# Chosen experts: where the next expert's turns and first products stand

## The reference

```python
xg = flat_x[topk_idx]
g = jnp.einsum('ecd,eid->eci', xg, Wg)
u = jnp.einsum('ecd,eid->eci', xg, Wu)
h = jax.nn.gelu(g, approximate=False) * u
eo = jnp.einsum('eci,edi->ecd', h, Wd)
eo = eo * topk_weight[..., None]
flat_out = jnp.zeros_like(flat_x).at[topk_idx.reshape(-1)].add(eo.reshape(-1, d))
```

## Time and profile before

| | |
|---|---|
| median of 3 executions | 4346.72 us (4342.63 to 4351.96) |
| the profiled execution: its own time | 4346.94 us |
| its span in the trace | 4345.3 us |
| TensorE matmuls busy | 3717.2 us, 86% of the span |
| VectorE busy | 2360.1 us, 54% |
| ScalarE busy | 1462.4 us, 34% |
| GpSimd busy | 1491.4 us, 34% |
| mean granted clock of TensorE | 0.915 of full speed |
| first turn of the chosen experts | 3586.20 us after the span's start |
| last down products of them begin | 4271.84 us |

### The profile page before, as it was taken

How to read it: one execution, slowest core, us unless ns; L and a number is a source line. 1 busy time by engine, 2 the same in 40 slices (tenths; PEclk the granted TensorE clock), 3 DMA queues, 4 the chain that set the end, 5 groups by cost and what they waited for, 6 DMA issues and landing times. The chain is left out here.

```text
span 4345.3 us, 55566 instructions
## 1 busy us (share of the span) xinstructions
PE 3717.2 (86%) x18610; PEld 1746.6 (40%) x18699; DVE 2360.1 (54%) x3948; ACT 1462.4 (34%) x2133; POOL 1491.4 (34%) x1279
## 2 busy tenths in 40 slices
PE   8989999998999689997699266476997989999994
PEld 3412222222333333333455255233555465555552
DVE  5579999964554135554722549655893661111113
ACT  2237777772333223333123124111452311111111
POOL 0042222234666216665156013133551322222221
PEclk9979999999999899999799576788997989999997
DMA  4543232311110431102422712233452113333323
GB/s 167 195 75 73 60 76 59 77 22 63 39 42 10 155 136 39 39 25 89 145 80 84 246 40 88 100 91 104 132 159 94 41 57 112 99 93 100 94 80 87
DMA packets 321435, 387.39 MB, mean 89 GB/s; under 512 B 56208, under 2 KB 248993, under 8 KB 319713
## 3 DMA queue, kind: packets, MB, share of 16 engines
q1 hardware_dynamic: 269376, 305.23, 22.5%
q0 software_dynamic: 31776, 57.19, 5.6%
q10 hardware_dynamic: 20096, 22.55, 1.5%
HBM read 240.68 MB, written 135.76 MB: 87 GB/s over the span
## 5 line engine op out<-in xcount | busy, mean ns | idle before, releaser
L590 DVE TENSOR_REDUCE modulated_mx<-modulated_ring 128x1 f32<-128x512 f32 x1024 | 651.4, 683 | 51.8 <-PE modulated_ring L497 45.9
L574 ACT ACTIVATE modulated_probs<-modulated_scores 128x1024 f32<-128x1024 f32 x512 | 496.1, 1021 | 181.5 <-PE modulated_scores L518 181.4
L2995 DVE TENSOR_TENSOR expert_h<-expert_gelu,expert_bank 128x512 f32<-128x512 f32 x128 | 88.1, 688 | 390.3 <-PE expert_bank L2963 387.5
L527 PE MATMUL modulated_acc<-modulated_probs,modulated_v 128*32 128x512 f32 x2048 | 273.6, 606 | 0.6 <-ACT modulated_probs L574 0.6
L497 PE MATMUL modulated_ring<-modulated_k,modulated_q 64*128 64x512 bf16 x1024 | 239.4, 399 | 34.1 <-DMA modulated_v<-scratch_v 23.0
L2923 POOL DMA_INDIRECT scratch_acc<-expert_y,expert_idx x64 | 101.1, 1580 | 482.2 <-DVE expert_y L3000 440.1
L518 PE MATMUL modulated_scores<-modulated_q,modulated_k 128*128 128x512 bf16 x945 | 255.6, 383 | 10.3 <-issue 5.4
L929 POOL TENSOR_TENSOR causal_total<-causal_total,causal_probs 128x1024 f32<-128x1024 f32 x96 | 225.7, 2351 | 86.9 <-ACT causal_probs L850 85.9
L929 POOL TENSOR_TENSOR meta_total<-meta_total,meta_probs 128x1024 f32<-128x1024 f32 x96 | 225.6, 2350 | 86.9 <-ACT meta_probs L850 85.9
L2963 PE MATMUL expert_bank<-expert_xT,expert_wg 128*128 128x512 f32 x512 | 243.2, 597 | 7.8 <-ACT expert_xT L2975 7.8
L872 DVE TENSOR_REDUCE meta_mx<-meta_maxima 128x2 f32<-128x1024 f32 x120 | 146.0, 1217 | 183.7 <-PE meta_maxima L756 183.7
(11 more groups left out here) (465 smaller groups left out, 6754.0 us busy)
## 6 DMA issues: line engine op xcount, KB each, us to landing
expert_wg<-x_WgT SPq DMA_DIRECT2D x16, 1024.0 KB, 4.9
expert_wu<-x_WuT SPq DMA_DIRECT2D x16, 1024.0 KB, 7.0
expert_wd<-x_WdT SPq DMA_DIRECT2D x16, 1024.0 KB, 5.2
modulated_k<-scratch_k_part SPq DMA_DIRECT2D x192, 64.0 KB, 2.9
modulated_q<-scratch_q_part SPq DMA_DIRECT2D x192, 64.0 KB, 3.0
scratch_v<-proj_v SPq DMA_DIRECT2D x8, 1024.0 KB, 6.5
modulated_v<-scratch_v SPq DMA_DIRECT2D x16, 512.0 KB, 4.5
scratch_M<-steps_snap SPq DMA_DIRECT2D x16, 512.0 KB, 3.2
```

The source lines that it names most:

```text
L527: last = nc.tensor.matmul(acc[32 * j:32 * j + 32, :], vs[g % SLOTS][:, t, j, :], probs[u % NPROBS][j // 2][:, j % 2, :], start=(t == 0), s ...
L574: nc.scalar.activation(probs[u % NPROBS][i][:], sc[i][:], ACT.Exp, scale=SCALE).then_inc(s_exp, 1)
L590: V.tensor_reduce(mx[h % 2][:, x // 2, 1 - j % 2, j // 2, x % 2:x % 2 + 1], ring[bank_of["max", 4 * m + j]][:], AX.X, ALU.max).then_inc(s_ ...
```

## The change

The jobs stand in another order. For each expert: g and u of f = 1 to 6; the other expert's turns; g and u of f = 7; the other expert's g 0 and u 0; the down products. For j = 1 "the other" is expert 0 of the next pair. What has no predecessor, the turns, g 0 and u 0 of expert 0, stands ahead of the loop; the last pair, which has no successor, is written out behind a loop of 7, with `tell` in the place of the missing jobs. `begin` gives the semaphores their credit up to the place in the list where that work starts.

```diff
         bank_of = lambda job: BANK[job[1]](job[2])
+        turns = lambda j: [(j, "turn", m) for m in range(KD)]
+        start_of = lambda j: [(j, "g", 0), (j, "u", 0)]
+        FIRST = turns(0) + start_of(0)
         jobs = []
         for j in range(2):
-            jobs += [(0, "turn", m) for m in range(KD)] if j == 0 else []
-            jobs += [(j, k, f) for f in range(FT) for k in ("g", "u")]
-
-            jobs += [(1, "turn", m) for m in range(KD)] if j == 0 else []
+            jobs += [(j, k, f) for f in range(1, FT - 1) for k in ("g", "u")]
+            jobs += turns(1 - j) + [(j, "g", FT - 1), (j, "u", FT - 1)] + start_of(1 - j)
             jobs += [(j, "d", a) for a in range(CT)]
+        LAST_D = [x for x in jobs if x[0] == 1 and x[1] == "d"]
+        lag = lambda x: int(x in FIRST)
+        spot = lambda steps: steps.names.index(next(x for x in FIRST if x in steps.names))
...
+        def begin(eng, steps):
+            eng.sem_inc(steps.sem, spot(steps))
+            steps.at = spot(steps)
...
-            def gather(i, j):
-
-                mm.wait(pool, i, (j, "turn", KD - 1), back=1)
+            def gather(i, j, first=False):
+                if not first:
+                    mm.wait(pool, i, (j, "turn", KD - 1), back=1 + int(j == 0))
...
+            begin(pe, mm)
+            for job in turns(0):
+                work(-1, job, 0, True)
+            act_s.wait(pe, -1, (0, "turn", KD - 1))
+            for kind in ("g", "u"):
+                mm.tell(pe, (1, kind, FT - 1))
+            for job in start_of(0):
+                work(-1, job, 0, True)
+            dve_s.wait(pe, -1, (0, "u", 0))
+            for job in LAST_D:
+                mm.tell(pe, job)
+            with pe.Fori(0, I_ - 1) as i:
+                for job in jobs:
+                    work(i, job, i + lag(job), False)
+            for job in jobs:
+                if job in FIRST:
+                    if job == (0, "turn", 0):
+                        dve_s.wait(pe, I_ - 1, (1, "u", FT - 2))
+                    if job == (0, "g", 0):
+                        dve_s.wait(pe, I_ - 1, (1, "u", FT - 1))
+                    mm.tell(pe, job)
+                else:
+                    work(I_ - 1, job, I_ - 1, False)
```

More of the change, by code:

```diff
@@ L2926, in scatter @@
                 freed[j].tell(pool, "y")
-            gather(0, 0)
+            gather(0, 0, first=True)
             with pool.Fori(0, I_ - 1) as i:
@@ L2940, in _ @@
             pe.wait_ge(s_made, 2)
[L2941 to L2953, removed]
-                    taken(before).wait(pe, i, before, back)
[L2955 to L2965, removed]
@@ new lines, in work @@
+            def work(i, job, e, ahead):
+                j, kind, m = job
+                out = bank[bank_of(job)]
+                if (kind, m) == ("turn", 0):
+                    gathered[j].wait(pe, e)
+                if (kind, m) == ("g", 0):
+                    act_s.wait(pe, i, (j, "turn", KD - 1))
+                    loaded[j].wait(pe, e)
+                if (kind, m) == ("d", 0):
+                    dve_s.wait(pe, i, (j, "u", FT - 1))
+                if not ahead:
+                    before, back = user_before(jobs, bank_of, jobs.index(job))
+                    taken(before).wait(pe, i, before, back)
+                if kind == "turn":
+                    for a in range(CT):
+                        last = nc.tensor.transpose(out[:, a * P:(a + 1) * P], xg[j][:, a, m * P:(m + 1) * P], ident[:])
+                elif kind == "d":
+                    for f in range(FT):
+                        last = nc.tensor.matmul(out[:, 0:D], h[j][:, f, m * P:(m + 1) * P], wd[j][:, f, :], start=(f == 0), stop=(f == FT - 1))
+                else:
+                    for kd in range(KD):
+                        last = nc.tensor.matmul(out[:], (wg if kind == "g" else wu)[j][:, kd, m * P:(m + 1) * P], xT[j][:, kd, :],
+                                                start=(kd == 0), stop=(kd == KD - 1))
+                mm.done(last, job)
@@ new lines, in work @@
+            def work(i, job, ahead):
+                j, kind, m = job
+                if kind == "turn":
+                    mm.wait(act, i, job)
+                    if not ahead:
+                        mm.wait(act, i, (j, "u", FT - 1), back=j)
+                    act_s.done(nc.scalar.activation(xT[j][:, m, :], bank[6 + m][:], ACT.Copy), job)
+                if kind == "g":
+                    mm.wait(act, i, job)
+                    if not ahead:
+                        before = (j, "u", m - 2) if m >= 2 else (1 - j, "u", FT - 2 + m)
+                        dve_s.wait(act, i, before, back=int((m >= 2 and j == 0 and m - 2 == 0) or (m == 1 and j == 0)))
+                    act_s.done(nc.scalar.activation(gel[m % 2][:], bank[m % 2][:], ACT.Gelu), job)
@@ new lines, in _ @@
+            begin(act, act_s)
+            for job in turns(0):
+                work(-1, job, True)
+            act_s.wait(act, -1, (0, "turn", KD - 1))
+            act_s.tell(act, (1, "g", FT - 1))
+            work(-1, (0, "g", 0), True)
+            with act.Fori(0, I_ - 1) as i:
+                for job in jobs:
+                    work(i, job, False)
+            for job in jobs:
+                if job in turns(0):
+                    if job == (0, "turn", 0):
+                        act_s.wait(act, I_ - 1, (1, "g", FT - 2))
+                    act_s.tell(act, job)
+                elif job != (0, "g", 0):
+                    work(I_ - 1, job, False)
```

41 lines of the change are left out of this document (27 added, 14 removed).

## The result

| | before | changed |
|---|---|---|
| median of 5 runs each, us | 4342.63 (4339.7 to 4351.96) | 4326.35 (4322.84 to 4330.98) |
| ratio, 95% interval | | 0.9959 (0.9945 to 0.9974) |
| profiled execution, span | 4345.3 | 4329.3 |
| first load of the stage issued to its last down products | 698.67 (3573.17 to 4271.84) | 682.71 (3574.19 to 4256.90) |
| granted clock, mean | 0.915 | 0.915 |

The stage is 15.96 us shorter in the trace, where 13.7 were predicted, and the span 16.0 us. The profiled execution of the changed kernel took 4330.98 us, the longest of its five.

The account below looks back on a forecast made before the run. TensorE was taken as the bound, with about 16 us idle. Gains of 16.4 less 2.6 at the edges and 0.1 for the gather made 13.7 us: 4346.94 - 13.7 - 0.2 = 4333.0, range 4328 to 4341.

Parts of the forecast that it names:

- Both stalls: TensorE's waits for xT copies ahead of gates (7.8 us gain) and expert_h ahead of down products (7.7 us) go.
- The pause ahead of the last pair's end: Last iteration: a wait for expert_h of f = 6 in the turns' place, 1.10 us plus 0.1 for increments.
- The gather's cover: Next gather ready 19.5 or 19.8 us after the down products' end, turns at 20.6; cover about 1 us.
- the one case at the edge: One gather ready 20.7 us after the down products' end, its turns due at 20.6; at most 0.1 us booked.
- The first loads' help: Prologue: asking for expert 1's weights after the first turns could gain 0 to 2.8 us; taken as 0.
- The clock: Rival: the prologue's new pause loses the risen clock again for 6 us, costing 3 us: 4336; chance 0.03.
- the rivals: Gather slightly late (0.07) or late enough to be slower (0.05), switches costing as much (0.09), clock falling in prologue (0.03).
- the switches: Rival: turns cost the full 1.11 us, up to down 0.2 per expert; net 9 us, 4338; chance 0.09.
- 4346.94 - 13.7 - 0.2 = 4333.0: Before's profiled time, less the net gain of 13.7 us, and 0.2 for lying above the median of 4346.72.
- A block of turns that nobody waits for: Eight turns on TensorE per expert, followed without a wait: between 0.88 and 1.11 us, taken as 1.00.
- The slow start behind a wait: Gate job behind the copies' wait takes 1.82 us in place of 1.72; 0.10 booked at seven boundaries.
- The prologue: Ahead of the loop TensorE waits for the first expert_h, 1.1 us, plus 0.3 for increments: 1.4 us.

Follow-up runs that it names:

- e1: Before with only the turns moved ahead of the last gate and up products; stage 696.54 us, median 4342.19 us, ratio to before 0.9999.
- e4: Changed kernel with counts added to the increment of the instruction before; stage 678.73 us, median 4322.95 us, ratio to before 0.9951.
- e9: e3 with wd's own semaphore and the even expert's wd asked for behind its turns; stage 674.77 us, median 4317.99 us.
- e3: Before with turns moved and the wait for the last expert_h at the eighth down matmul; stage 678.36 us, median 4320.20 us, ratio 0.9948.
- e2: Before with only the wait for the last expert_h moved to the eighth down matmul; stage 686.90 us, median 4333.37 us, ratio 0.9978.
- e5: Changed kernel, counts merged, no gate and up pair between turns and next gate; stage 697.27 us, median 4340.45 us, ratio to before 0.9994.
- e6: Changed kernel with an unused 128x1024 memset on GpSimd ahead of each gather; stage 682.88 us, 4327.11 us in one run.
- e7: Changed kernel with an unused 128x3072 memset on GpSimd ahead of each gather; stage 697.82 us, 4341.97 us in one run.

## Why the prediction was outside its range

**What held.** Both stalls went for the reasons given, and with 2.5 us to spare for each. The pause ahead of the last pair's end cost the 1.2 us booked. The gather's cover is what was worked out, and so is the one case at the edge (20.7 against 20.6; measured 20.65). The first loads' help did not come in this order. The clock never fell behind the prologue. None of the rivals happened: the switches cost less than the booked value, not more.

**The step that failed** is the last one, "4346.94 - 13.7 - 0.2 = 4333.0", with a range in which no term stands for the base. The 4346.94 of the profiled execution and the 4346.72 of three runs were taken as the kernel's level. Over 21 runs the same kernel has a median of 4342.72, and single runs lie between 4338.49 and 4349.16. The base was 4 us high, and the three values that I had (4342.63 to 4351.96) already lay 9.3 us apart. Of the 6.65 us between 4333.0 and the measured 4326.35, 4.1 are the base (4346.72 to the 4342.63 measured beside the changed kernel) and 2.6 the gain (16.3 by the medians, where 13.7 was forecast).

The reason for that scatter can be seen in part. The first load of the stage, behind work that neither kernel changes, is issued in the changed kernel here:

```profile
3574.19 0.32 SPq L188 DMA_DIRECT2D expert_idx_all<-scratch_idx  x1
```

The same row stands at 3573.17 in before, and in e1 to e4 at 3569.06, 3569.69, 3567.46 and 3567.08. That is 7 us between executions of one and the same code. Span less stage is 3646.6 us in the profiles of before and of the changed kernel, and 3639.5 to 3643.5 in those of e1 to e9, so the profiled execution of before was long outside the stage. It is not one wait alone: the same product of an earlier stage (top_h, L1587) starts on VectorE at 2212.75 in before, 2219.63 in the changed kernel and 2212.25 in e3, where the stage's first load comes 1.0 us later and 5.7 us earlier than in before. Which waits vary stays open.

**The terms that were mis-sized.** The net gain was 16.0 us in the stage, not 13.7:

- A block of turns that nobody waits for was taken as 1.00 us and is 0.87; the lower bound, 0.88 from the row's own spacing, was right. Times 15: 1.9 us. An estimate from the about 81 ns per matmul of 128 columns in the Trainium skill, page "TensorE: Matmul & The Clock Gate", section "Back-to-back issue gap", would be 0.65 us; the trace does not agree, with 0.11 us for each of the eight.
- The slow start behind a wait, 0.10 us, was booked for the gate only. The down products have it as well: their 13.91 fell to 13.81 at 15 boundaries, 1.5 us. Both numbers could be had from before: 13.91 exceeds 64 x 0.2145 = 13.73 by 0.18, and I used that excess as a price of the switch, for a rival, where half of it was the slow start that the change takes away.
- The prologue cost 2.2 us, not 1.4. The first gate waits 0.2 us longer (3.05 us from turns to gate in place of 2.82), from the end of expert_h to the next gate it is 0.84 us where 0.43 was booked, and expert_h starts 5.9 us behind the first gate where it started 5.75 behind: by the granted clock the rise to 2.4 GHz came 4.4 us behind that gate in place of 3.9.
- The last pair's second wait was 0.40 us dearer than the plain one, and 0.1 for a slow start.

1.9 + 1.5 - 0.8 - 0.5, and 0.15 for the earlier first turns, make 2.25, the difference of 15.96 to 13.7. Either error alone would have left the time in the range: 4346.72 - 16.0 is 4330.7, and 4342.63 - 13.7 is 4328.9. The same terms put the pair of experts at 84.7 to 84.9 us and the step from turns to gate at 0.9 to 1.1; they are 84.31 and 0.87. The range was too narrow because it was built from the bounds of the terms alone.

That the edges' cost is the counting is shown by e4, that the slow start goes with the wait by e2, and that the steady gain needs both moves, or a late wait in place of the second, by e1, e5 and e3.

## What to carry to other kernels

When work is reordered to hide a stall, list for each wait what covers it in the new order, and first ask whether the consumer can be made to wait later: here one moved wait that lets seven matmuls start before the last eighth of their operand is there gave 11.8 us, and with the turns moved it did as well as the changed order with its counts merged (678.36 and 678.73 us). Where a prologue has to count steps that it doesn't do, let the instruction before count them with a larger increment, since a wait made only to keep a count in order is a stall like any other. And a predicted time is a difference added to a base: take the base's scatter into the range, or predict against the median of many runs.

## What the runs showed of the hardware

- A matmul group ahead of which TensorE stood waiting for a semaphore takes about 0.10 us longer than one that follows without: 13.91 against 13.81 for 64 rows of 256 columns, 1.82 against 1.72 for four of 512 (the earlier trace rows and the timelines above). So a short stall costs its idle time and a tenth of a microsecond more.
- From the end of VectorE's product to TensorE's dependent matmul it is 0.12 to 0.13 us with a plain wait, 0.30 and 0.62 in the last pair of the changed kernel and 0.84 in its prologue, where increments without work stand between.
- The clock's rise at the stage's beginning did not stand at a fixed distance from the first work: by the granted clock in stretches of 2 us or less it lies 5.8 (e9), 6.7 (before), 7.5 (changed) and 8.1 us (e3) behind the first turns. What sets it is open. From turns to gate f = 1 the prologue takes 7.85 us in e9 and 9.00 in e3, whose steady parts are the same, and this limits what one trace can tell of an edge.
- Between a copy on GpSimd and the start of the indirect DMA that reads it 0.75 us pass in the changed kernel. A memset placed ahead of the last copy delayed the DMA by 0.60 us less than its own length, at 0.94 us of memset (e6) as at 2.65 (e7).
